# Loads in pieces, earlier scales, and two tiles copied in another order

## The reference

```
n    = layernorm(x)
q    = phi(n @ Wq.T);  k, v = split(ctx @ Wkv.T);  k = phi(k)    # phi(t) = t + 1 if t > 0 else exp(t); 16 heads of 32
attn = (q @ (k.T v)) / (q @ sum(k) + eps)                        # per head
x2   = x + (attn * sigmoid(n @ Wg.T + bg)) @ Wo.T
m    = layernorm(x2)
w, sel = top_k(m @ Wr, 2);  w = softmax(w)
out  = x2 + sum over the two chosen e of  w_e * (m @ We[e] + be[e])
```

## Time and profile before

| what | value |
| --- | --- |
| median of 3 runs | 557.02 us (555.86 to 558.27) |
| the profiled execution | 559.25 us, its span 557.7 us |
| PE busy | 523.0 us, 94% of the span |
| DVE, ACT, POOL busy | 305.6, 209.7 and 211.8 us |
| first transpose of a tile of the expert stage | 394.6 us |
| product of tile 0 added by DVE | 402.8 us |
| last add issued | 549.8 us |
| DMA moved | 92.93 MB |

### The profile page before, as it was taken

The page is one execution under the profiler, slowest core; times in us unless marked ns, Lnnn a source line. Parts: engine busy times, 40 slices in busy tenths (PEclk is TensorE's granted clock), DMA queues, the critical chain, the costliest instruction groups (busy, mean ns, idle before and its releaser), DMA issues.

```text
span 557.7 us, 12238 instructions
## 1 busy us (share of the span) xinstructions
PE 523.0 (94%) x4084; PEld 424.3 (76%) x4084; DVE 305.6 (55%) x918; ACT 209.7 (38%) x372; POOL 211.8 (38%) x235
## 2 busy tenths in 40 slices
PE   6999999899999999999999999999998879998990
PEld 5777788687778888777887878788876658886880
DVE  4483248637533773753377375377677675443440
ACT  6455432343443234344323444432442234333330
POOL 5342346521566032256603125300133563544353
PEclk9999999999999999999999999999999989999996
DMA  8912943551464225146422513679897988756855
GB/s 265 392 60 79 300 143 130 187 196 74 138 209 134 93 81 203 60 141 206 148 78 96 202 46 119 214 261 365 278 274 232 256 166 167 153 105 116 167 68 65
DMA packets 40873, 92.93 MB, mean 167 GB/s; under 512 B 4784, under 2 KB 4784, under 8 KB 40688
## 3 DMA queue, kind: packets, MB, share of 16 engines
q0 software_dynamic: 15184, 42.56, 28.7%
q1 hardware_dynamic: 24336, 47.22, 25.4%
q10 hardware_dynamic: 1296, 2.40, 1.3%
HBM read 53.81 MB, written 40.18 MB: 169 GB/s over the span
## 4 chain that ended last, share of the span: by engine, by line
PE 55%; DMA 16%; issue 7%; POOL 4%; POOLq 3%; DVE 1%; ACTq 1%; ACT 1%; DVEq 0%
PE pj L1133 15%; PE pj L1135 15%; PE pj L1134 15%; DMA out_dram<-khat,out_idx 8%; DMA out_dram<-buf,out_idx 6%; PE tp L1125 5%; PE pj L1220 2%; PE kvb L1192 2%; POOL aux L517 1%; DMA wraw<-in_L_ffn_We_dram 1%; POOLq L587 1%; POOL out_dram L592 1%; POOLq L586 1%; DMA we_halves<-aux 1%; PE pj L1142 1%
## 5 line engine op out<-in xcount | busy, mean ns | idle before, releaser
L1133 PE MATMUL pj<-R 128*128 128x512 f32 x448 | 184.5, 412 | 2.2 <-DVE R L794 2.2
L1135 PE MATMUL pj<-R 128*128 128x512 f32 x448 | 176.6, 394 | 0.0
L1134 PE MATMUL pj<-R 128*128 128x512 f32 x448 | 175.5, 392 | 0.0
L1133 PEld LDWEIGHTS pj<-R 128*128 128x128 f32 x448 | 84.9, 190 | 19.0 <-DVE R L794 3.8
L1135 PEld LDWEIGHTS pj<-R 128*128 128x128 f32 x448 | 84.6, 189 | 19.2
L1134 PEld LDWEIGHTS pj<-R 128*128 128x128 f32 x448 | 85.0, 190 | 15.3
L1133 PE MATMUL pj<-R,aux 128*128 x156 | 66.1, 424 | 9.5 <-DVE aux L798 4.5
L1135 PE MATMUL pj<-R,aux 128*128 x156 | 62.4, 400 | 0.0
L1134 PE MATMUL pj<-R,aux 128*128 x156 | 62.0, 397 | 0.0
L859 DVE SCALAR_TENSOR_TENSOR khat<-buf,khat 128x512 f32<-128x512 f32 x32 | 23.9, 747 | 59.2 <-ACT buf L663 57.6
L794 DVE TENSOR_TENSOR R<-tp,R 128x512 fp32r<-128x512 f32 x64 | 43.4, 683 | 16.4 <-ACT R L624 16.4
(11 more groups left out here) (198 smaller groups left out, 714.7 us busy)
## 6 DMA issues: line engine op xcount, KB each, us to landing
we_halves<-aux POOLq DMA_DIRECT2D x28, 512.0 KB, 4.7
R<-we_halves SPq DMA_DIRECT2D x6, 2048.0 KB
buf<-xs SPq DMA_DIRECT2D x34, 264.0 KB
buf<-in_ctx_dram SPq DMA_DIRECT2D x15, 512.0 KB, 4.5
wraw<-in_L_ffn_We_dram POOLq DMA_DIRECT2D x14, 512.0 KB, 5.6
wraw<-in_x_dram SPq DMA_DIRECT2D x4, 1024.0 KB, 8.7
out_dram<-gate SPq DMA_DIRECT2D x4, 1024.0 KB, 5.3
xs<-zeros POOLq DMA_DIRECT2D x4, 594.0 KB, 8.3
```

The source lines that it names most:

```text
L1133: nc.tensor.matmul(bank[:, :], s_hi(k), m_hi(k), start=(k == 0), stop=False)
L1134: nc.tensor.matmul(bank[:, :], s_hi(k), m_lo(k), start=False, stop=False)
L1135: last = nc.tensor.matmul(bank[:, :], s_lo(k), m_hi(k), start=False, stop=(k == KT - 1))
```

## The change

- First loads (SP): the context pair (0, 1) is issued ahead of Wq; `wr` and `bias` come only after the context pair (0, 2). DVE waits for these two small loads before the first gate and not before the first keys. The idle product on PE after the first transpose is 512 columns wide in place of 256.
- Pieces (SP): `load_halves` issues four DMAs of 512 KB for an expert; for expert 6 each waits until the one before has landed. Expert 7's low-numbered half comes as two DMAs, its other half as four of 256 KB, each after the one before has landed, with the loads of tiles 9 and 10 in between. The last batch's x2 is stored as four DMAs after the loads of tiles 11 to 14 in place of one after tile 10. `we_ready` counts 64 for an expert in place of 16.
- Scales (POOL): in the loop over batches the four x2 scales come before the first `cut_to_dram`, and the third cut comes after the scatters 0 and 1 and the next batch's x scale.
- Order of tiles (ACT and DVE): they walk through the list `LATE`, in which each "M" is put after the next "T" of a tile, so that tile m+2 is split before the result of tile m is handled. PE and POOL keep `START`.
- Banks: from tile 8 on products go round four banks; tiles 10 and 11 wait for the router's last use of theirs, tiles from 12 on for the copy of tile m-4.

```diff
--- before.py
+++ after.py
@@ -300,6 +300,21 @@
             START += tiles(m)
         START.remove(("T", "m", M_ALL))
 
+        LATE, due = [], []
+        for place_ in START:
+            LATE.append(place_)
+            if place_[:2] == ("T", "m"):
+                LATE += due
+                due = []
+            elif place_[0] == "M":
+                LATE.pop()
+                due.append(place_)
+        LATE += due
+
+        def m_bank(m):
+
+            return pj[m % (2 if m < 8 else 4)]
+
         block = stack.enter_context(nc.Block())
 
 
@@ -324,6 +339,10 @@
             def store_x2(b):
                 sp.wait_ge(SEMS["x2"], nth("x2", b, TT - 1))
                 sp.dma_start(out_rows[bass.ds(b * L, L), :].rearrange("(t p) d -> p t d", p=P), x2[:, :, :]).then_inc(x2_stored, 16)
+
+            def store_last(t):
+                sp.wait_ge(SEMS["x2"], nth("x2", B - 1, t))
+                sp.dma_start(out_rows[(B - 1) * L + t * P:(B - 1) * L + (t + 1) * P, :], x2[:, t, :]).then_inc(x2_stored, 16)
 
             def load_x(b):
                 sp.dma_start(x_raw, x[b, :, :].rearrange("(t p) d -> p t d", p=P)).then_inc(x_loaded, 16)
@@ -332,16 +351,16 @@
             load_w_chunks(WK)
             sp.dma_start(ctx_raw[:, 0, 1, :], ctx_in[0, P:2 * P, :]).then_inc(ctx_loaded[0], 16)
             load_w_chunks(WV)
-            sp.dma_start(wr_sb[:, :, :], wr.rearrange("(k p) e -> p k e", p=P)).then_inc(small_loaded, 16)
-            sp.dma_start(bias[:, :], bg.rearrange("(a d) -> a d", a=1).broadcast_to((P, D))).then_inc(small_loaded, 16)
+            ctx_pair(0, 1)
             load_w(WQ)
-            ctx_pair(0, 1)
             load_w(WG)
             sp.wait_ge(w_low, KT)
             load_w(WO)
             sp.wait_ge(w_low, 2 * KT)
             load_x(0)
             ctx_pair(0, 2)
+            sp.dma_start(bias[:, :], bg.rearrange("(a d) -> a d", a=1).broadcast_to((P, D))).then_inc(small_loaded, 16)
+            sp.dma_start(wr_sb[:, :, :], wr.rearrange("(k p) e -> p k e", p=P)).then_inc(small_loaded, 16)
             ctx_pair(0, 3)
             with sp.Fori(0, B - 1) as b:
                 ctx_pair(b + 1, 0)
@@ -359,20 +378,28 @@
                     sp.wait_ge(paid, m - XS + 1)
                 sp.dma_start(xs_raw[:, m % XS, :], xs_dram[bass.ds(row, P), :]).then_inc(xs_loaded[m % XS], 16)
 
-            def load_halves(e):
+            def load_halves(e, one_by_one=False):
 
                 sp.wait_ge(wx_stored, 32 * 2 * e)
-                sp.wait_ge(we_ready, 16 * e)
-                sp.dma_start(R[:, 2 * e:2 * e + 2, :, :].rearrange("p a k d -> p (a k) d").bitcast(F32),
-                             wx_dram[e, :, :, :].rearrange("a p d -> p a d")).then_inc(we_ready, 16)
-
-            def load_half(e, a):
-
-                if a:
-                    sp.wait_ge(we_ready, 16 * e)
-                    sp.wait_ge(half_loaded, 16)
-                sp.dma_start(R[:, 2 * e + a, :, :].bitcast(F32),
-                             wx_dram[e, a * KT:(a + 1) * KT, :, :].rearrange("k p d -> p k d")).then_inc(we_ready if a else half_loaded, 16)
+                sp.wait_ge(we_ready, 64 * e)
+                both_ = R[:, 2 * e:2 * e + 2, :, :].rearrange("p a k d -> p (a k) d")
+                for q in range(4):
+                    if q and one_by_one:
+                        sp.wait_ge(we_ready, 64 * e + 16 * q)
+                    sp.dma_start(both_[:, 2 * q:2 * q + 2, :].bitcast(F32),
+                                 wx_dram[e, 2 * q:2 * q + 2, :, :].rearrange("a p d -> p a d")).then_inc(we_ready, 16)
+
+            def load_last_low():
+
+                for q in range(2):
+                    sp.dma_start(R[:, 2 * E - 2, 2 * q:2 * q + 2, :].bitcast(F32),
+                                 wx_dram[E - 1, 2 * q:2 * q + 2, :, :].rearrange("k p d -> p k d")).then_inc(half_loaded, 16)
+
+            def load_last_high(q):
+
+                sp.wait_ge(we_ready, 64 * (E - 1) + 16 * q)
+                sp.wait_ge(half_loaded, 32)
+                sp.dma_start(R[:, 2 * E - 1, q, :].bitcast(F32), wx_dram[E - 1, KT + q, :, :]).then_inc(we_ready, 16)
 
             sp.wait_ge(SEMS["k"], nth("k", B - 1, ST - 1))
             load_halves(1)
@@ -382,7 +409,7 @@
             sp.dma_start(be_all[:, 0:4, :], be[0:4, :].rearrange("(a e) d -> a e d", a=1).broadcast_to((P, 4, D))).then_inc(be_loaded, 16)
             sp.wait_ge(SEMS["q"], nth("q", B - 1, G - 1))
             load_halves(3)
-            load_half(7, 0)
+            load_last_low()
             sp.wait_ge(planned, 1)
             for t in range(TT):
                 sp.wait_ge(scattered[t], 32 * (B - 1))
@@ -392,12 +419,17 @@
             load_halves(4)
             load_halves(5)
             sp.wait_ge(SEMS["wo"], nth("wo", B - 1, TT - 1))
-            load_halves(6)
-            load_half(7, 1)
-            for m in range(XS + 5, M0):
+            load_halves(6, one_by_one=True)
+            load_tile(9)
+            load_last_high(0)
+            load_last_high(1)
+            load_tile(10)
+            load_last_high(2)
+            load_last_high(3)
+            for m in range(11, M0):
                 load_tile(m)
-                if m == XS + 6:
-                    store_x2(B - 1)
+                if m < 11 + TT:
+                    store_last(m - 11)
             sp.wait_ge(planned, 2)
             for t in range(TT):
                 sp.wait_ge(scattered[t], 32 * B)
@@ -530,7 +562,7 @@
                 cut_first(k)
                 if k + 2 < KT:
                     load_first(k + 2)
-            pool.sem_inc(we_ready, 16)
+            pool.sem_inc(we_ready, 64)
             scale(0, 0, TT, "_x", 0, 0)
             pool.wait_ge(w_low, 5 * KT)
             load_expert(1, 0)
@@ -550,16 +582,16 @@
                 n_step[1:] = [per, b]
                 load_expert_at(2 * b + 2, 0)
                 load_expert_at(2 * b + 2, 1)
+                for t in range(TT):
+                    scale(1, t, 1, "_x2", b, t)
                 cut_to_dram(2 * b + 2, 0)
                 load_expert_at(2 * b + 3, 0)
                 cut_to_dram(2 * b + 2, 1)
                 load_expert_at(2 * b + 3, 1)
-                for t in range(TT):
-                    scale(1, t, 1, "_x2", b, t)
-                cut_to_dram(2 * b + 3, 0)
                 scatter(b, 0)
                 scatter(b, 1)
                 scale(0, 0, TT, "_x", b + 1, 0)
+                cut_to_dram(2 * b + 3, 0)
                 scatter(b, 2)
                 scatter(b, 3)
                 cut_to_dram(2 * b + 3, 1)
@@ -577,7 +609,7 @@
                 if m == 0:
                     pool.wait_ge(x2_stored, 16 * B)
                 if m == M0:
-                    pool.wait_ge(x2_stored, 16 * B + 16)
+                    pool.wait_ge(x2_stored, 16 * B + 16 * TT)
                 pool.wait_ge(MOE["y_copied"], mth(m))
                 if m == M0:
                     for d in range(1, YS):
@@ -745,7 +777,7 @@
                 act.wait_ge(paid, m - XS + 1)
                 act.dma_start(xs_raw[:, m % XS, :], xs_dram[bass.ds(row, P), :]).then_inc(xs_loaded[m % XS], 16)
 
-            for step, kind, i in START:
+            for step, kind, i in LATE:
                 if step == "T" and kind == "m":
                     high_m(i, i % 2)
                     if XS <= i + 3 < XS + 5:
@@ -918,6 +950,8 @@
                         next(planning, None) if b is LAST else None
                     elif step == "G":
                         if i == 0:
+                            if b == 0:
+                                dve.wait_ge(small_loaded, 32)
                             dve.wait_ge(x2_stored, b * 16 + 16)
                             dve.wait_ge(SEMS["x2n"], nth("x2n", b, -1))
                         dve.wait_ge(SEMS["g"], nth("g", b, i))
@@ -1069,7 +1103,6 @@
             low("c", 0, 0)
             for u in range(1, 2 * KT):
                 low_w(u)
-            dve.wait_ge(small_loaded, 32)
             dve.wait_ge(consts, N_CONSTS)
             keys(0, None)
 
@@ -1082,11 +1115,11 @@
 
                 dve.wait_ge(MOE["m_done"], mth(m))
                 dve.wait_ge(bias_gated, m + 1)
-                nc.vector.scalar_tensor_tensor(y_sb[m % YS], pj[m % 2][:, :], w_sel[:, m % (2 * YS):m % (2 * YS) + 1], y_sb[m % YS],
+                nc.vector.scalar_tensor_tensor(y_sb[m % YS], m_bank(m)[:, :], w_sel[:, m % (2 * YS):m % (2 * YS) + 1], y_sb[m % YS],
                                                ALU.mult, ALU.add).then_inc(MOE["y_copied"], 1)
 
             planning = plan_rest(bias[:, :])
-            for step, kind, i in START:
+            for step, kind, i in LATE:
                 if step == "T" and kind == "m":
                     low_m(i, i % 2)
                     pay(i)
@@ -1242,7 +1275,7 @@
             pe.wait_ge(pool_step, 3)
             pe.wait_ge(ctx_first, 16)
             turn("c", 0, 0, ctx_raw[:, 0, 0, :])
-            idle_product(D // 2)
+            idle_product(D)
```

(9 more changed lines are left out.)

## The result

| | before | after |
| --- | --- | --- |
| median (4 runs each) | 557.53 us (555.86 to 558.27) | 567.51 us (566.85 to 568.57) |
| profiled execution, span | 559.25, 557.7 us | 566.99, 565.5 us |
| ratio | | 1.0172, 95% interval 1.0129 to 1.0215 |

The account below looks back on a forecast made before the run. The chain of add landings in the expert stage was taken as the bound: -3.9 (earlier start) + 4.2 (later copies) - 4.7 (relief) = -4.4 us, cut to -3.0 by a late tile 11; 557.0 - 3.0 = 554.0 us, range 549.5 to 558.8.

Parts of the forecast that it names:

- I take 0.8, nearly one hit: a cut ran through just this place and PE did not wait: Keys stage: cost to PE of POOL's cuts newly placed there, 0.8 us taken, within 0 to 5.4.
- So PE should reach the expert stage 1.8 + 2.9 - 0.8 = 3.9 us earlier: Start of the expert stage: first loads and batch 0 gain, new cuts cost; bounds -1.7 and 5.0 us.
- the sign that I had named for "wrong": Expert stage: start under 2 us earlier, an add after tile 12 right behind its copy, or early adds still taking 8-9 us.
- the upper bound, 5.4: Keys stage: cost to PE if all six new cuts hit DVE, a full hit costing some 0.9 us.
- cuts hold DVE: Rival, keys stage: all six new cuts hit, 4.6 us more than taken, end at 558.6 us; chance 0.06.
- The start: First loads: PE's 0.80 us wait goes and the clock may rise sooner; 1.8 us gained, bounds 0.8 to 2.1.
- Batch 0: Batch loop: PE's waits of 1.66 and 1.23 us go with scales ahead of the cut; 2.9 us gained.
- The relief by itself: Expert stage: smaller loads shorten landings of add 2 to 6.5 us and add 4 to 5.5; 4.7 us gained.
- The later copies: Expert stage: copy 2 and add 2 come 4.2 us later; from tile 3 on the adds' distance covers it.
- Tile 11: Expert stage: its transpose, behind expert 7's last piece, taken at 442.7 us, making the gain -3.0 in place of -4.4.
- Add 5 thus moves by -3.9 + 4.2 - 4.7 = -4.4 us, and the rest follows at its old pace: Expert stage: earlier start, later copies and shorter landings together bring add 5, and the adds after it, 4.4 us earlier.

Follow-up runs that it names:

- plan_one_tile_earlier: The kernel after, with the pieces of the plan of the last tiles beginning at the copy of tile 7 instead of tile 8: 567.22 us, ratio 1.0176.
- own_copies_order: The kernel after, with ACT and DVE in the expert stage in the order of before and two banks for its products: 563.7 us, ratio 1.0104.
- late_copies_alone: The kernel before, with only the expert stage's order of copies and the four banks of after: 562.21 us, ratio 1.0106.
- no_cut_among_scatters: The kernel after, with both cuts of expert 2b+3 behind the last scatter: 557.62 us, ratio 1.0004.
- stores_behind_scatters: The kernel after, with the two stores of the first cut of expert 2b+3 issued behind scatter 3: 559.29 us, ratio 1.0024.
- scales_only_ahead: The kernel after, with the scales still ahead but the first cut of expert 2b+3 back ahead of scatter 0: 564.57 us, ratio 1.0146.

## Why the prediction was wrong

**The step that failed** is the sentence "I take 0.8, nearly one hit: a cut ran through just this place and PE did not wait", with the line that followed from it, "So PE should reach the expert stage 1.8 + 2.9 - 0.8 = 3.9 us earlier". What came is the sign that I had named for "wrong", a start of the stage less than 2 us earlier. Against the same loop without collisions (T0 389.43) the new order of cuts cost 8.4 us in the profiled execution of after, 7.7 of it in the three keys stages (from -4.5 to +3.2), and up to 11.5 in another (400.95); by medians, of different series, 9.9 (567.51 against 557.62) and 8.5 (563.7 against 555.17). Even the upper bound, 5.4, was too low, though only one khat per keys stage was hit: a hit cost PE 2.1 us where I had 0.9. Three errors lie in it.

First, the place that I had looked at shows no hold. This is what ran there beside the low half of the earlier trace rows:

```profile
110.84 0.81 DVE L859 SCALAR_TENSOR_TENSOR khat<-buf,khat 128x512 f32<-128x512 f32 x1 [1.85 <-ACT buf L663]
...
111.19 2.71 POOL L517 TENSOR_TENSOR aux<-wraw,aux 128x1024 fp32r<-128x1024 f32 x1
```

The step under the subtraction was the low half (111.58 to 112.26), one of whose two inputs lies in PSUM, and it took its usual 0.68 us; in no run did a low half that began under a subtraction take more than 0.69. Khat, with both inputs in SBUF, began just ahead of the subtraction. In the batch loop of before every khat that meets a cut begins ahead of its subtraction, and none takes more than 0.90 us; in after one falls into a subtraction in each of the three keys stages and takes 2.16, 2.37 and 2.00. That PE had not waited there was thus luck of the place, and said nothing of a khat under a subtraction. Second, I counted what a cut does to DVE, not what it does to the order on POOL: scatters 2 and 3 went out late and in a row, and ACT stalled beside them. Third, I took a wait of PE as its own price, while in some executions the half clock behind it added about 1.5 us (at the first of the three waits PE fell back by 3.9 us in `plan_one_tile_earlier` and 3.8 in `own_copies_order`, by 2.4 in after, with waits of 2.1 to 2.2 in all).

The rival "cuts hold DVE" named the right mechanism, with 0.06 and 558.6 us, because I took the missing waits in the profile of before as evidence about cuts in new places. The Trainium skill (SBUF — State Buffer, Who interferes with whom, and its section on the two sides) says that VectorE and GpSimd lock a pair of ports in turn, that a VectorE instruction with two inputs in SBUF needs it against a GpSimd instruction that reads SBUF, one with at most one such input outside the two-port modes does not, and that the first one keeps it for its whole instruction while the other stands still. The trace agrees: the router step of 0.17 us took 2.25, to the end of the subtraction, and the low half took 0.68. By that rule a step of 128x8 elements can cost as much as one of 128x512, so what counts is how many DVE steps with two inputs in SBUF stand under a cut, not their size.

**Right.** The start: 1.8 forecast, 1.6 seen. Batch 0: 2.9 forecast, 3.0 seen (-1.6 to -4.5). The relief by itself: 4.7 us forecast on the landings of adds 2 and 4, and 1.5 + 3.2 = 4.7 seen with the loads alone (6.4 and 5.6 us against 7.9 and 8.8); in after the landings were shorter by 2.8 + 1.4 (5.1 and 7.4). The later copies: 4.2 forecast, 4.6 seen at copy 2. Tile 11: forecast at 442.7, seen at 440.94, though the front was 7.1 us later than forecast; SP's first piece went out at 403.63 (403.1 forecast), so SP was faster than I took it.

**The second step that failed.** "Add 5 thus moves by -3.9 + 4.2 - 4.7 = -4.4 us, and the rest follows at its old pace": from T0 that is -0.5 for add 5, and over the eight runs with late copies and small loads it stood at 41.2 to 43.3, before at 42.3. The number is right in part by luck, because the two terms do not add as the sentence has it: `late_copies_alone`, with add 4 landing after 5.0 us in any case, has add 5 at 43.3, so there the 4.2 us of the copies cost 1.0, and the small loads beside late copies brought 0 to 2.1 and not 4.7. And the rest does not follow at its old pace. With the tile 11 that I took, the last add should have stood at 156.1 from T0; it stood at 159.8. By medians the loads give nothing at the end, and the later copies are not covered: in after, adds 11, 13 and 16 were issued 2.1 to 2.3 us behind their copies, the sign that I had named for "wrong". The late copies cost 5.3 us alone (562.21 against 556.88), 2.5 to 3.8 with the small loads. Where the relief is lost is not shown: from add 5 to the last add, runs with the loads of before took 112.9, 113.4 and 114.3 us and those with the small loads 114.4 to 118.7, and between adds 8 and 17 31.9 to 33.9 and 33.3 to 37.1, which points there but lies within the scatter of single executions.

Of the 13.5 us by which the forecast missed the median, 7.1 thus lie ahead of T0 and 3.7 behind it; the rest is how the two profiled executions stand to the medians.

**The sum by parts, from the runs:** start and scales without collisions -3.3 (554.88 against 558.16), cuts among the scatters +8.5 to +9.9, late copies +2.5 to +5.3, loads 0: between +7.7 and +11.9; measured +10.0.

**Open.** What stops ACT for 3.4 us (and PE for 1.2) isn't settled: the stall came only in runs where scatters left POOL late, it ended near the last of them, it shrank with a pause between them, and it did not depend on the stores. Code that arrives late is a rival that the traces do not decide: within the first stall of after (146.06 to 149.52) the DMA view counts one packet of an instruction queue, but one as well at the same place in `no_cut_among_scatters` (144.5 to 148), where ACT did not stop. Nor is it settled where the adds lose what the smaller loads gain, and what the late plan of the last tiles costs.

## What to carry to other kernels

An engine that works in order and whose long steps hold another engine's is a schedule of its own: before a long step is moved on it, list what stands behind it there and which steps run beside it on the other engine at the new place, and not at the old one. That no wait shows today may only say that no step of the kind that is held stands there today. A gain early in a chain of landings (4 us at add 5 here) is worth nothing until the chain behind it is shown to keep its pace; measure at the end of the chain.

## What the runs showed of the hardware

In the five runs in which POOL issued four scatter DMAs in a row at that place of the keys stage, ACT stopped for 4.2 to 4.9 us in each of the three stages, in one piece or two (3.45 and 0.97 in the first of after), and no semaphore in the trace explains it; over the first stop the DMA engines were 82% busy in after and 47% in `stores_behind_scatters`. With two in a row and a pause it stopped for 2.0. In `scales_only_ahead`, where four went out in a row earlier in the stage, ACT did not stop so, but PE did, for 1.2 us. After PE had waited 2.1 us, its granted clock was at half (1.2 GHz) for 3.4 us in some executions and not in others of the same code up to there: 0.51 and 1.00 over the same stretch, about 1.5 us of difference. Beside POOL's subtraction of 128x1024, a step of DVE of 128x8 elements took 2.25 us instead of 0.17 and a khat 2.00 to 2.37 instead of 0.69, while low halves of the same 128x512 with one input in PSUM took 0.68.
